# Two layers of attention and experts on one core: the front's buffers filled and loaded from other places, and the last stage's products turned

## What is computed

```
x = x + attention_0(layernorm(x))      # causal softmax attention, q, k, v and output weights 128 x 128
x = x + experts_0(layernorm(x))        # per batch the 2 best of 8 experts, 128 -> 512 -> 128, gelu, inner layernorm
x = x + attention_1(layernorm(x))      # each query keeps its 307 largest of 1024 scores, then softmax
x = x + experts_1(layernorm(x))        # below

def experts_1(x):                      # weights: w_gate, w_up (8, 128, 176), w_down (8, 176, 128)
    g = silu(x @ w_gate[e]) * (x @ w_up[e])        # for every expert e
    y = sum over e of combine[t, e] * (g @ w_down[e])   # combine: the 2 best of 8 per token, 0 for the others
    return y + (silu(x @ sw_gate) * (x @ sw_up)) @ sw_down   # shared part, 352 features
```

## Time and profile before

| | |
|---|---|
| median of 3 runs | 3681.74 us (3681.28 to 3684.51) |
| profiled execution, its time | 3686.02 us |
| profiled execution, its span | 3684.3 us |
| PE, DVE, ACT, POOL busy, share of the span | 75%, 75%, 68%, 53% |
| mean granted clock of PE | 0.771 |

### The profile page before, as it was taken

One profiled execution on the slowest core, in us unless ns is written; L12 is line 12 of the kernel. 1 busy time (PEld: TensorE's weight loads), 2 busy tenths in 40 slices (PEclk: granted clock), 3 DMA queues, 4 the chain that ended last, 5 costly groups with the idle time before them and its releaser, 6 DMA issues. The chain is left out here.

```text
span 3684.3 us, 83752 instructions
## 1 busy us (share of the span) xinstructions
PE 2778.2 (75%) x24345; PEld 1606.7 (44%) x24345; DVE 2745.3 (75%) x9136; ACT 2498.8 (68%) x4058; POOL 1953.7 (53%) x4541
## 2 busy tenths in 40 slices
PE   3399999667745777777777777776777777757999
PEld 2033333233423545444444544444454445445665
DVE  6677777235448988888888888887889888844444
ACT  2066666533128999989999989997889989832222
POOL 3023333410228777777777777776777777730000
PEclk9599999888656776777777766776666776777999
DMA  3111111000230101101100100110100110010000
GB/s 111 53 51 51 47 48 41 14 26 20 71 53 2 15 4 17 17 3 17 17 6 13 17 12 8 17 16 3 17 8 12 17 14 5 2 31 3 6 6 9
DMA packets 114079, 82.54 MB, mean 22 GB/s; under 512 B 57897, under 2 KB 97083, under 8 KB 113595
## 3 DMA queue, kind: packets, MB, share of 16 engines
q1 hardware_dynamic: 105403, 72.18, 9.1%
q0 software_dynamic: 8192, 4.79, 0.9%
HBM read 54.25 MB, written 19.40 MB: 20 GB/s over the span
## 5 line engine op out<-in xcount | busy, mean ns | idle before, releaser
L1125 PE MATMUL a_ST<-a_qs,a_ks 75*128 75x128 bf16 x4096 | 763.7, 275 | 302.8 <-ACT a_eT L1164 289.4
L1229 POOL TENSOR_TENSOR a_near<-a_side,a_z 128x1024 int32<-128x1024 int32 x512 | 968.6, 1892 | 43.8 <-POOL a_side L1225 2.1
L1327 DVE MAX8 a_cand<-a_near 128x8 f32<-128x256 f32 x2048 | 777.0, 405 | 3.3 <-POOL a_near L1229 2.5
L1125 PEld LDWEIGHTS a_ST<-a_qs,a_ks 75*128 75x128 bf16 x4096 | 510.9, 127 | 505.9 <-issue 454.6
L1366 DVE TENSOR_SCALAR_CACHE_REDUCE a_z<-a_S,a_thr 128x1024 f32<-128x1024 f32 x512 | 645.0, 1260 | 103.5 <-issue 81.5
L1149 ACT ACTIVATE a_signs<-a_z,a_tiny 128x1024 bf16<-128x1024 f32 x512 | 587.5, 1147 | 168.0 <-DVE a_z L1366 167.1
L1142 ACT ACTIVATE a_signs<-a_S,search 128x1024 bf16<-128x1024 f32 x512 | 569.3, 1112 | 35.8 <-PE a_S L1078 35.7
L1164 ACT ACTIVATE a_eT<-a_ST 128x1024 f32<-128x1024 f32 x512 | 518.7, 1013 | 69.5 <-PE a_ST L1126 68.7
L1078 PE MATMUL a_S<-a_ks,a_qs 72*128 72x512 bf16 x1024 | 442.4, 526 | 123.4 <-DVE a_z L1366 85.4
L717 ACT ACTIVATE a_eT<-a_ST 128x512 f32<-128x512 f32 (+3 forms) x768 | 354.3, 489 | 258.7 <-PE a_ST L687 198.9
L824 DVE TENSOR_REDUCE a_mx<-a_S 128x1 f32<-128x512 f32 (+3 forms) x768 | 380.8, 547 | 114.3 <-PE a_S L674 77.2
(11 more groups left out here) (340 smaller groups left out, 4617.1 us busy)
## 6 DMA issues: line engine op xcount, KB each, us to landing
a_qs<-q_parts SPq DMA_DIRECT2D x176, 64.0 KB
a_ks<-k_parts SPq DMA_DIRECT2D x176, 64.0 KB
a_qs<-a_flip SPq DMA_DIRECT2D x512, 0.8 KB
q_parts<-p_qp SPq DMA_DIRECT2D x48, 128.0 KB, 1.7
k_parts<-p_kp SPq DMA_DIRECT2D x48, 128.0 KB, 1.8
a_qs<-q_parts SPq DMA_DIRECT2D x64, 96.0 KB
a_ks<-k_parts SPq DMA_DIRECT2D x64, 96.0 KB
f_w<-L_ffn_W SPq DMA_DIRECT2D x16, 256.0 KB, 2.8
```

The source lines that it names most:

```text
L1125: pe.matmul(ST[:, block_of], ks[:, base(hl) + kb * P:base(hl) + (kb + 1) * P], qs[:, tile(hl):tile(hl) + P], start=True, stop=False)
L1229: pool.tensor_tensor(near[:, hl % 2, :].bitcast(I32), side[:, one].bitcast(I32).broadcast_to([P, SEQ]), z[:, hl % H, :].bitcast(I32), ALU. ...
L1327: mm = dve.max(found[:, 8 * g:8 * g + 8], near[:, h2 % 2, g * SW:(g + 1) * SW])
```

## The change

In `setup`, x has one semaphore per batch, and DVE computes the layernorm's statistics there, tile by tile as x arrives; POOL makes two constant tiles, `fill`, [128, 2048] of 0 and of 1. `project` for layer 0 receives mean and variance. Its loop over batches is written out for ACT and SP. SP issues the filler of `qs` and `ks` as transfers from the constant tiles, 4 of 256 KB per pass, ahead of each batch's stores. After the second batch's chunks ACT waits for the first batch's stores and pass 0's filler and issues the 16 transfers of pass 0 on its own queue; SP issues those of pass 1 after its last stores. The memsets of `attention0` are gone.

In `experts1`, Y has features in its rows: `wd` is the weights and 512 tokens of `gT` stream. So each chunk ends with a copy to SBUF (`lift`, DVE), 4 transposes (`turn`, PE) and the addition of x (`add`, DVE). The loops are written out, and a chunk's end lies among the next chunk's first pieces.

```diff
@@ setup
+        x_in = [sem(f"su_x_in{b}") for b in range(B)]
-                sp.dma_start(k.x[:, b * IB:(b + 1) * IB, :], xv[:, b * IB:(b + 1) * IB, :]).then_inc(loaded, 16)
+                sp.dma_start(k.x[:, b * IB:(b + 1) * IB, :], xv[:, b * IB:(b + 1) * IB, :]).then_inc(x_in[b], 16)
+            pool.memset(k.fill[0][:, :], 0.0)
+            pool.memset(k.fill[1][:, :], 1.0)
+            for b in range(B):
+                dve.wait_ge(x_in[b], 16)
+                for t in range(b * IB, (b + 1) * IB):
+                    dve.bn_stats(bn[:, t, :], k.x[:, t, :])
+                if b == 2:
+                    dve.wait_ge(loaded, 16 * len(loads))
+                    arrange()
+            dve.drain()
+            for t in range(NT):
+                dve.bn_aggr(mv[:, t, :], bn[:, t, :])
+            dve.drain()
+            dve.tensor_copy(ln0[0][:, :], mv[:, :, 0])
+            dve.tensor_scalar(ln0[1][:, :], mv[:, :, 1], LN_EPS, None, ALU.add)
@@ project, ACT
+            if layer == 0:
+                project_chunks(0)
+                project_chunks(1)
+                for c in range(CB):
+                    act.wait_ge(stored[c], free(1))
+                act.wait_ge(blank_s[0], 64)
+                load_pass0(act, k, 0)
+                project_chunks(2)
+                project_chunks(3)
@@ project, SP
+                def fill(x):
+                    for rows, odd in ((slice(64, P), 0), (slice(0, 64), 1)):
+                        cols = slice((2 * x + odd) * 2 * SEQ, (2 * x + odd + 1) * 2 * SEQ)
+                        for dst, const in ((k.qs, k.fill[0]), (k.ks, k.fill[1])):
+                            sp.dma_start(dst[rows, cols], const[rows, :]).then_inc(blank_s[x], 16)
+                fill(0)
+                store(0)
+                fill(1)
+                store(1)
+                fill(2)
+                store(2)
+                fill(3)
+                store(3)
+                sp.wait_ge(blank_s[1], 64)
+                load_pass0(sp, k, 1)
+                sp.wait_ge(blank_s[2], 64)
+                sp.wait_ge(blank_s[3], 64)
+def load_pass0(queue, k, x):
+    for e in range(2):
+        cols = slice(first + e * 2 * SEQ, first + (e + 1) * 2 * SEQ)
+        for u, n in ((0, 3), (1, 3), (2, 2)):
+            at = 64 * e + u * SPLIT * HD
+            queue.dma_start(k.qs[at:at + n * HD, cols], pair_of(k.q_parts[u, at_x, :], e).broadcast_to([n, HD, 2 * SEQ])).then_inc(arrived, 16)
+            queue.dma_start(k.ks[at:at + n * HD, cols], pairs_of(k.k_parts[0:n, at_x, :], e)).then_inc(arrived, 16)
...
@@ attention0, SP and DVE
-            sp.wait_ge(kones_s, 1)
-            load(0)
             load_v(0)
-            load(1)
             sp.wait_ge(kq_in[0], 16 * DMAS_Q)
-            load(2)
+            load_pass0(sp, k, 2)
-                dve.memset(by_head(qs), 0.0)
-                dve.memset(by_head(ks), 1.0)
@@ experts1, PE
-                            for t in range(CT):
-                                mm = pe.matmul(Y_ps[c][:, t, :], gT[0:ROWS[i], (c * NP_ + i) % RINGS, t * P:(t + 1) * P],
-                                               wd[0:ROWS[i], i, :], start=(i == 0 and t == 0), stop=(i == NP_ - 1 and t == CT - 1))
+                    pe.matmul(Y_ps[n % CB][:, :], wd[0:ROWS[i], i, :], gT[0:ROWS[i], g % RINGS, :],
+                              start=(i == 0), stop=(i == NP_ - 1)).then_inc(down, 1)
+                def turn(n):
+                    pe.wait_ge(yT_s, n + 1)
+                    for t in range(CT):
+                        mm = pe.transpose(Y_ps[n % CB][:, t * P:(t + 1) * P], yT[n % CB][:, t * P:(t + 1) * P], k.ident[:, :])
+                    mm.then_inc(turned, 1)
+                for g in range(ALL + 2):
+                    if g < ALL:
+                        project_piece(g)
+                        if g % NP_ == TURN_AT and g >= NP_:
+                            turn(g // NP_ - 1)
+                    if g >= 2:
+                        sum_piece(g - 2)
+                turn(NCH - 1)
@@ experts1, DVE
+                def lift(n):
+                    dve.wait_ge(down, (n + 1) * NP_)
+                    if n >= CB:
+                        dve.wait_ge(turned, n - CB + 1)
+                    dve.tensor_copy(yT[n % CB][:, :], Y_ps[n % CB][:, :]).then_inc(yT_s, 1)
```

More of the change, by code:

```diff
@@ L105, in build @@
         k.b1T = sb("b1T", [P, E0 * FC0])
-        setup(nc, k, inp)
         ln1 = [ctx.enter_context(nc.sbuf_tensor(f"ln1_{x}", [P, NT], F32)) for x in ("mean", "var")]
         with ExitStack() as part:
-            project(nc, k, 0, None)
-            ctxT = part.enter_context(nc.sbuf_tensor("ctxT", [P, 4, SEQ], F32))
             packed = part.enter_context(nc.sbuf_tensor("packed", [D, TOK], F32))
-            attention0(nc, k, ctxT, packed)
+            with ExitStack() as front:
+                ln0 = [front.enter_context(nc.sbuf_tensor(f"ln0_{x}", [P, NT], F32)) for x in ("mean", "var")]
+                k.fill = [front.enter_context(nc.sbuf_tensor(f"fill_{x}", [P, 2 * SEQ], BF16)) for x in ("zero", "one")]
+                setup(nc, k, inp, ln0)
+                k.qs, k.ks = (front.enter_context(nc.sbuf_tensor(f"a0_{x}", [P, 4 * G0 * SEQ], BF16)) for x in ("qs", "ks"))
+                k.kq_in = [front.enter_context(nc.semaphore(f"a0_kq_in{c}")) for c in range(2)]
+                project(nc, k, 0, None, ln0)
+                ctxT = front.enter_context(nc.sbuf_tensor("ctxT", [P, 4, SEQ], F32))
+                attention0(nc, k, ctxT, packed)
             experts0(nc, k, inp, packed, ln1)
@@ L203, in _, with arrange @@
         def _(dve):
[L204 to L210, removed]
+            def arrange():
+                for x in range(4):
+                    paired = lambda a: a[:, 32 * x:32 * x + 32].rearrange("p (a e d) -> p e d a", a=2, e=2)
+                    in_order = lambda a: a[:, 32 * x:32 * x + 32].rearrange("p (e d a) -> p e d a", e=2, a=2)
+                    dve.tensor_copy(in_order(rows), paired(raw_rows)).then_inc(kept, 1)
+                    for s, w in enumerate((k.wq[0], k.wk[0])):
+                        dve.tensor_copy(in_order(w), paired(raw_qk[:, s, :]))
+            for b in range(B):
[11 more added lines that the diff above has]
+            dve.tensor_scalar(ln0[1][:, :], mv[:, :, 1], LN_EPS, None, ALU.add)
             dve.wait_ge(pe_done, 1)
@@ L275, in project @@
             first, step, base1 = search
+        blank_s = [sem(f"blank{x}") for x in range(4)] if layer == 0 else None
         block = ctx.enter_context(nc.Block())
@@ L488, in _, with store @@
                 sp.nop().then_inc(stored[c], 1)
-            with sp.Fori(0, B) as b:
+            def store(b):
                 for c in range(CB):
@@ new lines, in _ @@
+                for g in range(ALL):
+                    n, i = divmod(g, NP_)
+                    rows, held = slice(0, ROWS[i]), gate
+                    dve.wait_ge(silu, g + 1)
+                    if i < NE:
+                        if g >= 2:
+                            dve.wait_ge(prod, g - 1)
+                        dve.tensor_tensor(weighed[:, g % 2, :], W_ps[g % 2][:, :], gate[:, g % 2, :], ALU.mult).then_inc(wd_s, 1)
+                        dve.wait_ge(wd_s, n * NE + i + 1)
+                        held = weighed
+                    if g >= RINGS:
+                        dve.wait_ge(down, g - RINGS + 1)
+                    dve.tensor_tensor(gT[rows, g % RINGS, :], U_ps[g % 2][rows, :], held[rows, g % 2, :], ALU.mult).then_inc(prod, 1)
+                    if n > 0 and i == LIFT_AT:
+                        lift(n - 1)
+                    if n > 0 and i == ADD_AT:
+                        add(n - 1)
@@ L1984, in route1 @@
+                lift(NCH - 1)
+                add(NCH - 1)
 def route1(nc, k, xT, weight, owner, loads, loaded, topk_scale):
```

153 lines of the change are left out of this document (67 added, 86 removed).

## The result

The changed kernel takes 3639.33 us, the median of 4 runs (3635.95 to 3645.47), against 3683.12 (3681.28 to 3684.99) for the kernel before in the same comparison: ratio 0.9883, 95% interval 0.9866 to 0.9900. It is faster by 1.2%, and 2.7 us from the forecast of 3642.

The account below looks back on a forecast made before the run. Bound: 48.4 us before attention0's first maximum, filled only by one engine's memsets, then one load; PE in experts1. 3686.0 - 38.1 - 2.0 = 3645.9; the profiled execution stands 4.3 above the median, so 3642; range 3631 to 3655.

Parts of the forecast that it names:

- Statistics in setup: Front: three batches' statistics hide under the loads, so ACT's root comes 11.7 us earlier; bounds 10 and 13.
- Pass 0 from ACT's queue: Projection: ACT's 16 issues delay the fifth chunk's `xT` by 9.8 us, taken as 10.0; bounds 0 and 17.
- Filler as transfers: Projection: filler transfers fit in the free half of the DMA engines; cost 0, up to 5 us.
- last store's issue to first maximum: Into attention0: memsets -25.0, load -20.7, pass 1's issues +10.6, landing no longer awaited -1.4, rounding 0.1.
- first maximum: Start of attention0: DVE's first maximum at 106.9 instead of 145.04, 38.1 us earlier; forecast wrong if outside 97 to 121.
- experts1: Last stage: 0.45 us less per chunk, -3.6 for 8, new steps at the end +1.6; sum -2.0, bounds -4 to +3.
- the 26 to 28 that I gave as a sign: Front: ACT's root of the variance was to stand at 26 to 28 us.
- the first rival: Projection: ACT's issues hold nothing up, 9.8 us more gained, 3632; chance 0.12.
- the second: Both loads' issues slow, 1.10 us each: +14, 3656; half of it gives 3649; chance 0.17 for the two.
- the upper bound: Filler in the projection: up to 5 us if the DMA engines lack room and a chunk's buffers come free late.
- the slower rival: experts1: PE's wait for DVE's lift costs its clock, a chunk's 39 us become up to 78; chance 0.03.
- The start of attention0: With pass 0 landed and no memset, PE starts at once and the first maximum stands 1.4 us behind.

Follow-up runs that it names:

- e3: The changed kernel with pass 0's transfers issued by SP after its last stores, ahead of pass 1's, and none by ACT: 3642.23 us, ratio 0.9876.
- e4: The changed kernel with pass 0's transfers issued by ACT after its last chunk: 3634.31 us, ratio 0.9858.
- e7: The changed kernel with rows of `qs` and `ks` permuted, so the 12 large transfers of each pass have outermost dimension 8: 3615.09 us, ratio 0.9802.
- e6: The changed kernel with the filler of all four passes issued ahead of the first stores: 3637.18 us, one run.
- e1: The changed kernel with `experts1` of the kernel before, so the front's edits alone: 3642.59 us, ratio 0.9878.
- e2: The kernel before with `experts1` of the changed kernel, nothing else: 3681.14 us, ratio 0.9985.
- e5: The kernel before with only the statistics moved into `setup`, without the filler: 3671.55 us, one run.
- e10: The kernel before with only the rows of `qs` and `ks` permuted for outermost dimension 8: 3651.78 us, ratio 0.9904.
- e8: The changed kernel with e7's rows, pass 0 issued by ACT after its last chunk, and pass 1 by SP behind the barrier: 3602.20 us, ratio 0.9769.

## Why the prediction was right, and where it was not

By its own terms, from the two profiled executions:

| term | forecast | measured |
|---|---|---|
| *Statistics in setup* (the root) | -11.7 | -13.1 |
| *Pass 0 from ACT's queue* (fifth `xT`, beside the root) | +10.0 | +8.6 |
| *Filler as transfers* (fifth chunk's v waits for a store) | 0, up to 5 | +5.0 |
| PE at half clock after its pauses | not in the sum | +3.6 |
| last store's issue to first maximum | -36.4 | -36.7 |
| **first maximum** | **-38.1** | **-32.6** |
| *experts1* | -2.0 | -2.9 |
| attention1 | 0 | -7.1 |
| between, and the end | 0 | +2.0 |
| **sum** | **-40.1** | **-40.6** |

*Statistics.* The mechanism held: three batches lie under the loads (DVE is done with them at 10.2), and only the fourth and the aggregates stand behind the weights. The root, at 25.4, is ahead of the 26 to 28 that I gave as a sign. The term was mis-sized by 1.4, for the 32 aggregates took 2.22 us, not the 3.0 of the earlier trace rows, and the 12 copies 0.085 apart.

*Pass 0 from ACT's queue.* The pause is 9.73 us for a forecast of 9.8 against the old start. The issues themselves took longer, 49.37 to 61.33 is 12.0, but the first 2.3 us ran beside the last ACTIVATEs. So the first rival (issues beside ACTIVATEs) was true for 2.3 us of 12, and the second (issues at 1.10 each) for the first three, at 0.72 to 1.52. SP's 16 for pass 1 took 10.5, as forecast.

*Filler as transfers* is the step that failed. It named the chunk, the fifth, and its predecessor's stores, and then said that this chunk "is held by ACT anyway". ACT holds it for 9.7 us, the stores for 5 more. The size is that of the upper bound, but the reason behind the bound, filler that fills the DMA engines, is not what the runs show. What makes the stores late is the load from ACT's queue, for which the prediction counted issues alone. The third chunk's stores of k land within 16.3 us in after; without a load beside them within 2.2 with the filler ahead of them (e3, and e4, where v waits 0.55), and within 1.8 without filler (before); with the load's rows in the new order within 5.4 (e7). In e6 a store in the middle of the load takes 11.4 us with no filler about. Whether the filler adds to the 16.3 is not shown. I had weighed the DMA share, which is a mean over 16 engines. My reading is that the load keeps a few engines busy and that the stores need these too; no run shows which engines a transfer used, nor how they share their work.

*The clock* was a term for experts1 in the slower rival and for nothing at the front. After ACT's pause PE runs at half clock: q and k of the fifth chunk took 2.08 and 1.92 us (0.7 later up to v). The last four chunks' 2.9 come with the second pause, the store's: in e6 and e7, which have ACT's pause and not the store's wait, these chunks have their clock of 0.88 and take 25.1 and 25.5 us. So the failed step cost 5.0 + 2.9 = 7.9 us; e7, without it, is 7.3 earlier.

*The start of attention0* went as written: no memset, pass 0 landed, scores 0.6 us behind the last issue, and the gain kept as far as the first output product of layer 0, 732.9 before and 700.3 after, again 32.6.

*experts1.* Forecast 0.45 a chunk, measured 0.52 (39.43 to 38.91), and the steps new at the end, from the lift to the addition, took 1.4 instead of 1.6 (3638.85 to 3640.29). The clock held; the slower rival did not occur.

*attention1* is the same code in both kernels, and yet 7.1 shorter. Nine kernels with the same stage spread over 13 us, so I take it for scatter between programs. e1 and e3 lie between the two, e6 at 2131.2, and the three kernels with the old front, before, e2 and e5, at 2138.8 to 2140.0, above the six others. That hints at a cause, which stays open. A part of it lies in the search, which takes 23.9 us in before and 22.3 in after; without the search the old front (e10, 2111.9) and the new one (e7 and e8, 2110.8 and 2110.2) are within 2 us.

So the forecast hit by cancellation, which is luck: at the front it promised 5.5 us more than came; experts1 gave 0.9 more than forecast, and stages that it held unchanged gave 5.1.

## What to carry to other kernels

Before transfers are moved in among others, look at the shape of each one, not only at how busy the DMA engines are on average: a load with an outermost dimension of 2 or 3 held a store back for 16.3 us at a mean share of 0.44, where full engines without it let the store land in 2.2. Put issues where their engine has ended its work in the stage; in the middle they cost their own length, and a wait that follows from them can cost PE its clock. And compare only programs with the same data-dependent branches: one search of 22 us came or went with the order of a sum.

## What the runs showed that I had not expected

- The time of an issue depends on what else is in flight: the fourth chunk's three stores of q took SP 9.30 us in after, 2.00 in e7 and 1.53 in e3.
- ScalarE's queue began the first of its 16 issues at 49.37, while the first of the four ACTIVATEs ahead of it in the list was running; the last of them ended at 51.71.
- The same load of 16 transfers took 20.1 us with an outermost dimension of 2 or 3 in 12 of them, and 13.1 with 8, its issues alone being 10.5.
